# Forward substitution in the second attention layer: probabilities as the stationary operand, one product per later block, one chain in place of two half chains

## The chip, the core and the metric

The kernel runs on one core of one Trainium2 chip. The metric is the device time of one execution in microseconds (us). All of it is one program: two attention layers, a ternary feed-forward layer and a mixture of eight experts, for 4 sequences of 256 tokens with 256 channels. The engines are named as in the profile: PE (TensorE, with PEld for its weight loads), DVE (VectorE), ACT (ScalarE), POOL (GpSimd) and SP (SyncE, here the DMA queue).

## The reference, cut to the part that is changed

The change lies in the second attention layer. It has 16 heads of 16 channels. Besides the usual softmax attention it solves one lower triangular system per head and sequence:

```python
beta = hidden_states @ Wb + bb
s = einsum('bihd,bjhd->bhij', k, k) * scale          # keys against keys
s = where(strict, s, -inf)                           # j < i only
p = e / denom                                        # softmax over j < i
L = p * beta.transpose(0, 2, 1)[..., None]
A = L + eye(T)
u = solve_triangular(A, v, lower=True)               # T = 256 rows, 16 channels
attn = softmax(causal q k^T * scale)
o = einsum('bhij,bhjd->bihd', attn, u)
return o @ Wo
```

So `u = v - L u` in the strictly lower part: row i of `u` needs all earlier rows.

## The kernel before

**Blocks.** The 256 rows are cut into `NS` = 8 blocks of `BLK` = 32. The 128 partitions hold 4 groups of 32 rows (`HQ` = 4, index `hh`), and the free dimension holds 4 heads (`Q4` = 4, index `q`), so a tile of 128 x (4 x 16) is one block of `u` for all 16 heads. Each group of 32 partitions uses its own 32 x 32 tile of the PE array, so four products run side by side.

**What is prepared for a sequence b.** `kscores` makes the key scores in 5 groups, DVE takes their maxima and ACT turns them into sums of exponentials (`ncc`, later `-beta / sum`). `kdiag` makes the diagonal blocks, and POOL inverts all of them in the step `blocks` (lines 1968 to 1984, 62 small operations one after another). DVE transposes the inverses into `invT` in the step `inverse` (line 1754). `kprobs` makes the unnormalised probabilities `later[b % 2][s]`: for block s, keys of that block on partitions, all later queries (7 blocks down to 1) on the free axis. `vproj` makes the right-hand side `vz`.

**The substitution.** For s = 0 to 7 the step `solve` multiplies the inverse of diagonal block s with the right-hand side `zz` (16 products of 32x32 by 32x16), and DVE copies the result from PSUM into `ublk`. Then the step `update` adds the contribution of block s to all later blocks at once: `ublk` is the stationary operand, and `later` streams through with (7 - s) x 32 columns, down from 224 to 32 (line 1104). The result lies in PSUM with channels on partitions, so DVE first transposes the next block's piece (line 1762) and then, head by head, multiplies by `ncc` and adds `vz` (line 1765, four operations). Both steps are split into two halves of two heads each (`half`), which follow each other on PE and DVE. A solution block goes by 4 DMAs from `ublk` to `uaug` (line 831), which `pv` needs complete.

**PSUM.** Each step's PSUM banks come from three rings. `solve` takes turns with `max` and `kmax` in the ring "small" (banks 6 and 7). The running updates lie in banks 4 and 5, one per half.

**Order.** Engines run in the order of `ORDER`, and DVE in `DVE_ORDER`. `make_order` spreads other work (`ahead[b]`: queries, key scores, probabilities and output projection of neighbouring sequences) over the 15 places between the steps of the substitution. The function `lag` lets DVE do a step of the substitution first and the other step that stood ahead of it afterwards. After the substitution of sequence b come `pv` (attention times `u`), then `otr`, `oT`, `wo` (two transposes and the output projection), which are part of the next sequence's spread work. The inversion on POOL for sequence b + 1 starts behind `inverse` for b, since DVE runs `den` and `blocks` for b + 1 there.

## Time and profile before

| | us |
|---|---|
| median of 3 runs (845.45 to 848.48) | 846.26 |
| the profiled execution, its own time | 847.45 |
| its span in the trace | 845.6 |
| first substitution with the work around it | 445.9 to 502.2 |
| move of the last block, first `pv` of the layer | 502.2 to 522.7 |
| second substitution | 522.7 to 579.4 |
| third substitution, POOL inverts the blocks of the last sequence | 579.4 to 628.6 |
| last substitution | 628.6 to 654.7 |
| rest of the layer, experts, output | 654.7 to 845.6 |

The time that the table's first line gives is what is measured from run to run; the trace belongs to the one profiled execution. Its span leaves out 1.85 us around the program. In the rows below, a time is counted from the start of the span. In a row of the timeline, several like instructions that follow each other are merged (x32 is their count), and a matmul on fp32 data stands for two records, so 16 products are x32.

### The profile page before, as it was taken

The page shows a single profiled execution, that of the slowest core. Times are in us where ns is not written, and L with a number is a line of the kernel's source. Part 1 is how long each engine was busy: PE and PEld are TensorE (multiplying, and loading weights), DVE is VectorE, ACT ScalarE, POOL GpSimd, SP SyncE. Part 2 cuts the span into 40 slices and gives each one's busy share as a digit, 9 for nine tenths or more (in the row PEclk, how much of TensorE's full clock was granted, in tenths as well). Part 3 has the DMA queues.
Part 4 walks back from the last instruction along what each step waited for, and adds up shares of the span by engine and source line. Part 5 has one row for each costly group of instructions (what it writes and reads, how often), then busy time and mean ns, then how long its engine had stood idle before and what let it go on. Part 6 is the DMA issues. An engine that isn't in the chain of part 4 may idle for free. (4 is left out here: it accounts for less than half of the span.)

```text
span 845.6 us, 17910 instructions
## 1 busy us (share of the span) xinstructions
PE 506.5 (60%) x7444; PEld 419.3 (50%) x7444; DVE 552.5 (65%) x1066; ACT 299.8 (35%) x716; POOL 227.6 (27%) x320
## 2 busy tenths in 40 slices
PE   0333256288695866426466465758877660899980
PEld 0332144266484645325354344546655450899970
DVE  6549789687699796776627763556564155667733
ACT  3222535244354630053650332442313150365520
POOL 2000000000000000103855826813850026044343
PEclk9865568699788967757677676857979655899995
DMA  8255001404000010760070014200001062656214
GB/s 312 91 112 112 1 1 32 81 1 102 12 2 1 1 50 1 158 143 4 2 151 7 8 43 79 46 6 9 10 9 12 5 276 80 250 193 234 84 52 124
DMA packets 52067, 61.30 MB, mean 72 GB/s; under 512 B 25409, under 2 KB 45393, under 8 KB 47505
## 3 DMA queue, kind: packets, MB, share of 16 engines
q1 hardware_dynamic: 50176, 55.15, 24.2%
q0 software_dynamic: 1808, 4.99, 2.0%
q8 instruction: 59, 0.97, 0.5%
q14 instruction: 24, 0.19, 0.1%
HBM read 45.24 MB, written 13.63 MB: 70 GB/s over the span
## 5 line engine op out<-in xcount | busy, mean ns | idle before, releaser
L873 PE MATMUL psum<-arena 32*32 32x16 f32 (+17 forms) x5608 | 351.3, 269 | 257.3 <-DVE arena L1544 67.1
L873 PEld LDWEIGHTS psum<-arena 128*32 128x32 f32 (+7 forms) x5608 | 279.3, 127 | 328.3 <-DVE arena L1544 70.7
L1979 POOL TENSOR_TENSOR arena<-arena 128x31 f32<-128x31 f32 (+15 forms) x124 | 69.1, 558 | 9.7
L1977 POOL TENSOR_TENSOR arena<-arena 128x31 f32<-128x31 f32 (+15 forms) x124 | 63.6, 513 | 9.7
L1615 DVE TENSOR_REDUCE arena<-psum 128x2 f32<-128x512 f32 (+1 forms) x48 | 41.4, 861 | 21.5 <-PE psum L873 21.1
L1335 ACT ACTIVATE psum<-psum,arena 128x256 f32<-128x256 f32 (+7 forms) x128 | 45.8, 371 | 22.2 <-DVE arena L1605 22.2
L1957 POOL DMA_DIRECT2D arena<-wq x1 | 0.9, 862 | 191.7 <-PE psum L873 191.7
L1304 ACT ACTIVATE arena<-psum 128x512 f32<-128x512 f32 (+1 forms) x48 | 35.3, 735 | 47.0 <-PE psum L873 46.9
L1514 DVE TENSOR_TENSOR_SCAN arena<-arena 128x255 f32<-128x255 f32 x64 | 42.5, 727 | 9.6 <-ACT arena L1247 9.4
L1990 POOL TENSOR_TENSOR fc_second_parts<-arena,fc_first_parts 128x2048 fp32r<-128x2048 f32 x6 | 27.9, 4654 | 63.7 <-ACT fc_first_parts L1425 63.7
L1412 ACT ACTIVATE psum<-psum,arena 128x256 f32<-128x256 f32 x64 | 24.8, 458 | 48.1 <-PE psum L873 48.1
L1762 DVE STREAM_TRANSPOSE arena<-psum 128x64 f32<-128x64 f32 x56 | 13.8, 246 | 42.7 <-PE psum L1104 42.3
L1425 ACT ACTIVATE fc_first_parts<-arena 128x2048 fp32r<-128x2048 f32 x16 | 30.4, 1919 | 26.6 <-PE psum L873 26.6
L1247 ACT ACTIVATE arena<-arena 128x255 f32<-128x255 f32 x64 | 27.2, 500 | 34.9 <-DVE arena L1500 34.9
L1500 DVE TENSOR_TENSOR_SCAN arena<-arena 128x256 f32<-128x256 f32 x64 | 39.0, 671 | 0.4
L873 PE MATMUL psum<-input_first_parts,fc_first_parts 128*128 128x256 f32 x128 | 37.2, 291 | 2.6 <-DVE input_second_parts L1865 1.5
L873 PE MATMUL psum<-fc_first_parts,hidden_first_parts 128*128 128x256 f32 x128 | 36.9, 288 | 2.7 <-DVE hidden_second_parts L1883 2.7
L1997 POOL DMA_INDIRECT dispatched<-arena x16 | 20.3, 1267 | 67.4 <-DVE arena L1830 62.8
L1970 POOL TENSOR_TENSOR arena<-arena 128x1024 f32<-128x1024 f32 x4 | 7.7, 1913 | 110.6 <-DVEq L1747 110.6
L873 PE MATMUL psum<-input_first_parts,fc_second_parts 128*128 128x256 f32 x128 | 36.9, 288 | 0.0
L873 PE MATMUL psum<-input_second_parts,fc_first_parts 128*128 128x256 f32 x128 | 36.9, 288 | 0.0
L1104 PE MATMUL psum<-arena 32*32 32x224 f32 (+6 forms) x896 | 35.9, 307 | 1.5 <-DVE arena L1776 1.5
(180 smaller groups left out, 955.7 us busy)
## 6 DMA issues: line engine op xcount, KB each, us to landing
arena<-fc SPq DMA_DIRECT2D x16, 1024.0 KB, 5.2
arena<-parts SPq DMA_DIRECT2D x40, 256.0 KB, 4.6
parts<-arena SPq DMA_DIRECT2D x16, 384.0 KB, 3.3
arena<-parts SPq DMA_DIRECT2D x40, 128.0 KB, 5.6
dispatched<-arena SPq DMA_DIRECT2D x1, 2048.0 KB, 19.0
arena<-arena SPq DMA_DIRECT2D x128, 8.0 KB, 1.8
arena<-dispatched SPq DMA_DIRECT2D x8, 256.0 KB, 3.1
expert_rows<-arena SPq DMA_DIRECT2D x8, 256.0 KB, 2.2
```

The costliest lines, as they stand in the source:

```text
L873: return nc.tensor.matmul(out, lhsT, rhs, start=start, stop=stop)
L1104: last = nc.tensor.matmul(acc(half)[rows, qq, (s + 1) * BLK:T], ublk[rows, s, q, :], later[b % 2][s][rows, q, :], start=s == 0 and qq == 0 ...
L1247: A(scan[s + 1][:, ct, 0:T - 1], scan[s][:, ct, 0:T - 1], ACT.Copy, scale=back[:, i:i + 1]).then_inc(scaled, 1)
L1304: step_(A(prob[:, hs, 0:T], hi, ACT.Exp, scale=scale))
L1335: ins = A(s_, s_, ACT.Exp, bias=nbias[:, n:n + 1], accum_out=ncc[b][:, n:n + 1])
L1425: A(w_parts[i][e % 2][0][:], fcw[e % NW][i], ACT.Copy).then_inc(w_first, 1)
L1500: ins = V.tensor_tensor_scan(scan[s][:, ct, :], dd, src[:, ct, bt(b)], 0.0, ALU.mult, ALU.add)
L1514: st(V.tensor_tensor_scan(scan[s][:, ct, T - 2::-1], dd, scan[s + 1][:, ct, T - 2::-1], scan[s][:, ct, T - 1:T], ALU.mult, ALU.add))
L1615: st(V.tensor_reduce(mneg[:, H + j * n:H + (j + 1) * n], hi, axis=AX.X, op=ALU.max, negate=True))
L1977: link(G_.tensor_tensor(tmp, A3[:, k + 1:BLK, k:k + 1].to_broadcast([P, rows, w]), X3[:, k:k + 1, 0:w].to_broadcast([P, rows, w]), ALU.mult))
L1979: ins = G_.tensor_tensor(X3[:, k + 1:BLK, 0:w], X3[:, k + 1:BLK, 0:w], tmp, ALU.add)
L1990: G_.tensor_tensor(second[:], fcw[e % NW][1], first[:].bitcast(F32), ALU.subtract).then_inc(w_second[1], 1)
```

## The change

The substitution keeps its blocks and its order of steps, but is formulated the other way around. An `update` for a block is now 16 small products with `later` (32x32) as the stationary and `ublk` (32x16) as the streamed operand, so the result already lies as the solution does, and the transposes go. The update for the next block (s + 1) is made at once; those for the later blocks t > s are made behind `solve` of step s, from block s - 1. The right-hand side is no longer added on DVE: PE multiplies the inverse with `vz` as soon as the update is issued and adds the inverse times the scaled update afterwards in the same PSUM columns (bank 5). DVE is left with one multiplication and one copy per block, each over all four heads. The two half chains become one. `solve` no longer takes part in the ring "small", and `ublk` is 16 columns wide per head instead of 32, without its zeroed half.

```diff
-    ("solve", None): ("small", ("dve",)),
...
-        solve = [[("inverse", b)] + ([("den", b + 1), ("blocks", b + 1)] if b + 1 < B else []) + [("solve", b, 0, 0), ("solve", b, 0, 1)]]
+        solve = [[("inverse", b)] + ([("den", b + 1), ("blocks", b + 1)] if b + 1 < B else []) + [("solve", b, 0)]]
         for s in range(1, NS):
-            solve += [[(kind, b, s - (kind == "update"), half) for half in range(2)] for kind in ("update", "solve")]
+            solve += [[("update", b, s - 1)], [("solve", b, s)]]
...
+            def add_block(b, s, t):
+
+                for q in range(Q4):
+                    for hh in range(HQ):
+                        rows = slice(hh * BLK, (hh + 1) * BLK)
+                        at = (t - s - 1) * BLK
+                        last = nc.tensor.matmul(acc[rows, t, q, :], later[b % 2][s][rows, q, at:at + BLK], ublk[rows, s, q, :],
+                                                start=s == 0 and t == 1 and q == 0, stop=True, skip_group_check=True)
+                return last
+
+            def inverse_of(b, s, first, rhs):
+
+                for q in range(Q4):
+                    n = s * Q4 + q
+                    for hh in range(HQ):
+                        rows = slice(hh * BLK, (hh + 1) * BLK)
+                        last = nc.tensor.matmul(sol[rows, s, q, :], invT[b % 2][rows, n * BLK:(n + 1) * BLK], rhs[rows, q, :],
+                                                start=first and q == 0, stop=True, skip_group_check=True)
+                return last
...
                 elif kind == "update":
 
-                    _, b, s, half = step
-                    wait_done(pe, ("solve", b, s, half), "dve")
+                    _, b, s = step
+                    pe.wait_ge(u_ready, sol_count(b, s))
                     if s == 0:
                         wait_done(pe, ("kprobs", 1, b, KP - 1), "act")
-                        if b == 0:
-                            pe.wait_ge(pad_ready, 1)
-                    for qq in range(QP):
-                        q = half * QP + qq
-                        for hh in range(HQ):
-                            rows = slice(hh * BLK, (hh + 1) * BLK)
-                            last = nc.tensor.matmul(acc(half)[rows, qq, (s + 1) * BLK:T], ublk[rows, s, q, :],
-                                                    later[b % 2][s][rows, q, :], start=s == 0 and qq == 0, stop=True,
-                                                    skip_group_check=True)
-                    last.then_inc(acc_written, 1)
+                    add_block(b, s, s + 1).then_inc(acc_written, 1)
+                    inverse_of(b, s + 1, True, vz[b][:, s + 1])
                 elif kind == "solve":
...
                     else:
-                        pe.wait_ge(z_ready, z_count(b, s, half))
-                    slot = acquire(step)
...
+                        pe.wait_ge(z_ready, z_count(b, s))
+                        inverse_of(b, s, False, zz).then_inc(solved, 1)
+                        for t in range(s + 1, NS):
+                            add_block(b, s - 1, t)
...
                 elif kind == "update":
 
-                    _, b, s, half = step
-                    qs = slice(half * QP, (half + 1) * QP)
-                    dve.wait_ge(acc_written, upd_count(b, s, half))
-                    link(V.transpose(accn[:, qs], acc(half)[:, :, (s + 1) * BLK:(s + 2) * BLK]))
-                    for q in range(half * QP, (half + 1) * QP):
-                        n = (s + 1) * Q4 + q
-                        ins = V.scalar_tensor_tensor(out=zz[:, q], in0=accn[:, q, 0:HD], scalar=ncc[b][:, n:n + 1],
-                                                     in1=vz[b][:, s + 1, q], op0=ALU.mult, op1=ALU.add)
...
+                    _, b, s = step
+                    dve.wait_ge(acc_written, upd_count(b, s))
+                    scale = ncc[b][:, (s + 1) * Q4:(s + 2) * Q4].unsqueeze(2).to_broadcast([P, Q4, HD])
+                    V.tensor_tensor(zz, acc[:, s + 1], scale, ALU.mult).then_inc(z_ready, 1)
                 elif kind == "solve":
-                    _, b, s, half = step
-                    slot = filled(step)
+                    _, b, s = step
+                    dve.wait_ge(solved, sol_count(b, s))
                     if b and s == 0:
                         dve.wait_ge(u_moved, 16 * HQ * NS * b)
-                    give_back(step, V.tensor_copy(ublk[:, s, half * QP:(half + 1) * QP, 0:HD],
-                                                  single(slot)[:, 0:QP * HD].rearrange("p (q e) -> p q e", q=QP)))
+                    V.tensor_copy(ublk[:, s], sol[:, s]).then_inc(u_ready, 1)
```

PE, last substitution (b = 3), from the first update to the second, before. L1104 is the update, L1047 the transposes of `otr`, `32x16` the product with the inverses, and the four rows 128x256 to 128x128 x5 are a group of probabilities:

```order
L1104 MATMUL psum<-arena 32x224 x16
L1047 MATMUL psum<-arena 128x128 x8
L873 MATMUL psum<-arena 32x16 x16
L873 MATMUL psum<-arena 128x256
L873 MATMUL psum<-arena 128x128
L873 MATMUL psum<-arena 128x256
L873 MATMUL psum<-arena 128x128 x5
L1104 MATMUL psum<-arena 32x192 x16
```

The same stretch of PE after the change. L886 is `add_block`, L896 `inverse_of`:

```order
L886 MATMUL psum<-arena 32x16 x16
L896 MATMUL psum<-arena 32x16 x16
L1069 MATMUL psum<-arena 128x128 x8
L896 MATMUL psum<-arena 32x16 x16
L886 MATMUL psum<-arena 32x16 x96
L875 MATMUL psum<-arena 128x256
L875 MATMUL psum<-arena 128x128
L875 MATMUL psum<-arena 128x256
L875 MATMUL psum<-arena 128x128 x5
L886 MATMUL psum<-arena 32x16 x16
```

Six products per head and group (x96) now stand between the second `solve` and the second update; the number falls to 80, 64, 48, 32 and 16 in the steps that follow.

DVE, the end of the last substitution, before, from the copy of block 6 to the copy of block 7 (L1657 and L1544 are the end of `wo` and the gate that follows it):

```order
L1776 COPY arena<-psum 128x2x16 x2
L1762 STREAM_TRANSPOSE arena<-psum 128x64
L1765 SCALAR_TENSOR_TENSOR arena<-arena 128x16 x2
L1762 STREAM_TRANSPOSE arena<-psum 128x64
L1765 SCALAR_TENSOR_TENSOR arena<-arena 128x16 x2
L1657 TENSOR_TENSOR arena<-psum,arena 128x2x256
L1544 SCALAR_TENSOR_TENSOR arena<-arena 128x2x256
L1776 COPY arena<-psum 128x2x16 x2
```

The same stretch of DVE after the change:

```order
L1779 COPY arena<-psum 128x64
L1773 TENSOR_TENSOR arena<-psum,arena 128x64
L1668 TENSOR_TENSOR arena<-psum,arena 128x2x256
L1555 SCALAR_TENSOR_TENSOR arena<-arena 128x2x256
L1779 COPY arena<-psum 128x64
```

The two transposes and four products of a block became one operation, and the other work kept its place.

## Rows read from the trace of the kernel before

**Rows 1.** Engines by stage: window in us, then each engine's busy us (x instructions), granted clock
```profile
445.90:502.20 56.30, 35.37 (x946) 26.04 (x946) 40.20 (x113) 13.02 (x68) 37.05 (x65) 0.70 0.06 7
522.70:579.40 56.70, 37.76 (x1001) 28.64 (x989) 31.84 (x104) 22.25 (x87) 27.97 (x50) 0.72 0.13 21
579.40:628.60 49.20, 39.07 (x870) 29.49 (x870) 30.22 (x89) 13.85 (x29) 37.77 (x66) 0.83 0.08 9
628.60:654.70 26.10, 22.18 (x564) 16.56 (x564) 13.23 (x63) 7.74 (x18) 0.00 (x0) 0.93 0.11 11
```

**Rows 2.** Chain that ended last, by line, in 445.9:502.2, 522.7:579.4 and 628.6:654.7
```profile
by line: PE psum L873 16.0%; ACT psum L1335 15.6%; PE psum L1104 14.0%; DVE arena L1765 8.7%; DVE arena L1615 5.3%; DMA parts<-arena 4.9%; DVE arena L1596 4.3%; DVE arena L1762 3.7%; DVE arena L1754 3.4%; issue 3.2%; DVE arena L1745 3.2%; D
...
by line: PE psum L873 32.7%; ACT psum L1335 12.1%; PE psum L1104 10.4%; DVE arena L1765 9.6%; DVE arena L1596 6.3%; issue 5.5%; DVE arena L1762 4.7%; DVE arena L1615 3.3%; PE psum L1047 1.9%; ACT arena L1349 1.8%; DVE arena L1616 1.8%; DVE 
...
by line: PE psum L873 35.9%; PE psum L1104 21.4%; DVE arena L1765 14.8%; DVE arena L1762 8.5%; DVE arena L1754 7.6%; PE psum L1047 3.9%; issue 3.5%; DVE arena L1544 2.7%; ACT arena L1258 2.4%; PE psum L1057 2.4%; DVE arena L1657 2.3%; DVE a
```

**Rows 3.** The same chain piece by piece: start us, us, what; one block of b = 3
```profile
644.13 0.99 PE psum L873 x24
645.12 0.40 PE psum L1104 x16
645.52 0.02 issue
645.54 0.26 DVE arena L1762
645.80 0.03 issue
645.83 0.38 DVE arena L1765 x2
646.21 0.17 DVE arena L1762
646.38 0.03 issue
646.40 0.39 DVE arena L1765 x2
646.79 0.04 issue
646.84 3.86 PE psum L873 x24
```

**Rows 4.** Timeline of PE: start us, us, instruction xcount, [idle before <-releaser]
```profile
451.08 3.21 PE L1104 MATMUL psum<-arena 32*32 32x224 f32 x32 [1.34 <-DVE arena L1776]
629.38 1.72 PE L1104 MATMUL psum<-arena 32*32 32x224 f32 x32 [0.20 <-DVE arena L1776]
559.09 0.41 PE L873 MATMUL psum<-arena 32*32 32x16 f32 x16
640.73 0.31 PE L873 MATMUL psum<-arena 32*32 32x16 f32 x16 [0.35 <-DVE arena L1765]
504.67 1.60 PE L873 MATMUL psum<-arena 98*32 98x32 bf16 x136 [2.74 <-DVE arena L1565]
562.17 2.65 PE L873 MATMUL psum<-arena 32*32 32x16 f32 x32 [2.67 <-ACT arena L1294]
623.34 4.32 PE L873 MATMUL psum<-arena 128*32 128x256 f32 x64 [0.35 <-issue]
```

**Rows 5.** Durations by line on DVE: x count, ns min/median/max
```profile
L1776 DVE COPY arena<-psum x64: 173/191/193, 450.8 to 654.5; 128x32 f32<-128x32 f32 x64
...
L1723 DVE TENSOR_TENSOR arena<-psum,arena x8: 164/169/175, 343.4 to 507.0; 128x16 f32<-128x16 f32 x8
...
L1562 DVE TENSOR_TENSOR arena<-psum,arena x8: 681/692/693, 334.3 to 502.4; 128x512 f32<-128x512 f32 x8
```

**Rows 6.** Timeline of POOL and DVE: the inversion for the last sequence, first and last pieces
```profile
584.52 1.91 POOL L1970 TENSOR_TENSOR arena<-arena 128x1024 f32<-128x1024 f32 x1 [30.01 <-DVEq L1747]
...
626.66 1.98 DVE L1754 STREAM_TRANSPOSE arena<-arena 128x1024 f32<-128x1024 f32 x1 [4.04 <-POOL arena L1979]
```

**Rows 7.** Chain that ended last, end of the first stage to the first pv
```profile
502.18 2.77 DMA parts<-arena
...
512.11 5.66 DMA arena<-arena
517.77 0.09 issue
517.86 4.21 PE psum L873 x64
```

**Rows 8.** Timeline of SP: the DMAs that move the last block
```profile
654.71 2.52 SPq L831 DMA_DIRECT2D arena<-arena  x4
```

**Rows 9.** Windows around the wait for POOL: columns as in rows 1
```profile
619.50:626.60 7.10, 4.63 (x52) 3.13 (x54) 2.80 (x7) 0.27 (x1) 6.00 (x15) 0.51 0.08 10
...
628.60:631.00 2.40, 2.11 (x64) 1.29 (x64) 0.90 (x6) 0.16 (x1) 0.00 (x0) 1.00 0.04 3
```

**Rows 10.** Groups by line, DVE: x count | busy us, mean ns | idle before, releaser
```profile
L1765 DVE SCALAR_TENSOR_TENSOR arena<-arena 128x16 f32<-128x16 f32 x112 | 27.1, 282 | 2.0
L1762 DVE STREAM_TRANSPOSE arena<-psum 128x64 f32<-128x64 f32 x56 | 13.8, 246 | 42.7 <-PE psum L1104 42.3
L1776 DVE COPY arena<-psum 128x32 f32<-128x32 f32 x64 | 10.6, 187 | 25.7 <-PE psum L873 25.3
```

More of the change, by code:

```diff
@@ L325, in lag @@
         o.append(step)
-        if step[0] == "solve" and step[2] == NS - 1 or not solving:
-            solving = solving and step[-1] == 0
-        if step[0] in ("update", "solve") and step[-1] == 1 or not solving:
+        if step[0] == "solve" and step[2] == NS - 1:
+            solving = False
+        if step[0] in ("update", "solve") or not solving:
             o += held
@@ L625, in later_cols, with per_block @@
             return block_cols(slot, T - (g + 1) * BLK, T - (s + 1) * BLK)
-        def acc(half):
-            return psum[:, 4 + half, :].rearrange("p (q i) -> p q i", q=QP)
+        def per_block(bank):
+            return psum[:, bank, :].rearrange("p (s q e) -> p s q e", s=NS, q=Q4)
+        acc, sol = per_block(4), per_block(5)
         def single(slot):
@@ L822, in _ @@
                     sp.dma_start(wvb[:, :, :, Q4 * HD:VB], d["wb"].rearrange("p c (h n) -> p c h n", h=HQ)).then_inc(loaded["wv1"], 16)
-                elif kind == "solve" and step[3] == 1:
-                    _, b, s, _ = step
+                elif kind == "solve":
+                    _, b, s = step
                     t, r = divmod(s, NB)
-                    for half in range(2):
-                        wait_done(sp, ("solve", b, s, half), "dve")
+                    sp.wait_ge(u_ready, sol_count(b, s))
                     if b and s == 0:
@@ L1112, in _ @@
                         wait_done(pe, ("vproj", b), "act")
-                    else:
-                        pe.wait_ge(z_ready, z_count(b, s, half))
-                    slot = acquire(step)
-                    for qq in range(QP):
-                        q = half * QP + qq
-                        n = s * Q4 + q
-                        for hh in range(HQ):
-                            rows = slice(hh * BLK, (hh + 1) * BLK)
-                            rhs = zz[rows, q, :] if s else vz[b][rows, 0, q, :]
-                            last = mm(single(slot)[rows, qq * HD:(qq + 1) * HD], invT[b % 2][rows, n * BLK:(n + 1) * BLK], rhs)
-                    wrote(step, last)
+                        if b:
+                            pe.wait_ge(u_ready, sol_count(b - 1, NS - 1))
+                        inverse_of(b, 0, True, vz[b][:, 0]).then_inc(solved, 1)
+                    else:
+                        pe.wait_ge(z_ready, z_count(b, s))
+                        inverse_of(b, s, False, zz).then_inc(solved, 1)
+                        for t in range(s + 1, NS):
+                            add_block(b, s - 1, t)
                 elif kind == "route":
@@ L1346, in _ @@
                     else:
-                        wait_pe(act, ("solve", b, NS - 1, 1))
+                        act.wait_ge(solved, sol_count(b, NS - 1))
                         act.wait_ge(invT_ready, b + 1)
```

29 lines of the change are left out of this document (13 added, 16 removed).

## The prediction

> **What bounds the kernel now.** I read the windows by stage first. No engine is full in the stages that hold a substitution: PE is busy 35.4 of 56.3 us in the first and 37.8 of 56.7 us in the second, DVE 40.2 and 31.8 us [rows 1]. Such stages are bound by turns between engines, so the chain of waits decides. Its shares by line [rows 2] give what the substitution holds of each stage, as update (L1104), transpose (L1762) and scale-and-add (L1765) together:
> - first stage: 14.0 + 8.7 + 3.7 = 26.4% of 56.3 = 14.9 us
> - second: 10.4 + 9.6 + 4.7 = 24.7% of 56.7 = 14.0 us
> - last: 21.4 + 14.8 + 8.5 = 44.7% of 26.1 = 11.7 us
>
> The rest of the chain is queries, key scores and probabilities on PE (L873), ACT's exponentials over key scores (L1335) and DVE's maxima (L1596, L1615). It stays.
>
> The third stage is another case. POOL starts to invert the last sequence's blocks at 584.52, and DVE waits 4.04 us for it until 626.66 [rows 6]. Ahead of it stand only two transposes of DVE (about 2 us each). A faster third substitution ends earlier and waits longer, so the 49.2 us of this stage stay, and nothing is gained in it. The way from the first substitution to the first pv is a chain of DMAs (2.77 us of storing, loads, then 5.66 us until the moved block lands behind them) and is not touched either [rows 7]: it only starts earlier. For the first and second sequence POOL is not late: an inversion takes 42 us (584.5 to 626.6) [rows 6], and the stages are 56 us long.
>
> **Price of a product.** 8 products of 32x32 by 32x16 took 0.41 us at 559 and 0.31 us at 640; the 224-column update took 3.21 and 1.72 us [rows 4]. The granted clock around the two cheap ones was 0.93 to 1.00 (2.4 GHz), in the other stages it was mixed, 0.70 and 0.72 [rows 1, 9]. Read as twice the pace and a fixed end, 8 products are 0.10 us + 0.21 at 2.4 GHz and 0.20 + 0.21 at 1.2 GHz. So 16 products that somebody waits for are 0.41 (0.62) us, and 16 that merely stand in the row 0.21 (0.42) us. All 28 narrow products of a sequence are 5.9 us at 2.4 GHz. The seven old updates were 896 columns, at 1.49 us for 224, so 6.0 us. **PE saves nothing.** It even pays for the right-hand side, 7 x 0.21 = 1.5 us per sequence, which lies beside DVE's scaling. What changes is where the work stands. On the chain a block now has only its first product; the far ones (6, 5, 4, 3, 2, 1, in all 21) stand behind the solve, where DVE copies for about 0.4 us. What exceeds that is on the chain when the next step has nothing else to wait for.
>
> A page disagrees. The Trainium skill, "TensorE: Matmul & The Clock Gate", section "Wait — 56ns, not 53.3ns?", says that matmuls never start less than about 25 ns apart, however narrow. By that the 32 records of 16 products would be 0.8 us instead of 0.21. The row of 16 records in 0.31 us speaks against it for products on four tiles of the array [rows 4], and the new ones are of the very same form, so the row is taken.
>
> An upper bound in a long run is the row of 136 records in 1.60 us, 12 ns each [rows 4]: 0.38 us for 16 products. That row has other shapes (98 rows, bf16), the row of like form is nearer, and I take 0.21 and 0.42 and keep 0.38 for the range at 2.4 GHz. Below 0.21 there is no row.
>
> **Price of the scaling.** One DVE operation from PSUM on 64 columns: 16 columns took 169 ns, 512 columns 692 ns, so about 0.22 us [rows 5]. With its wait some 0.25 us, in place of two transposes and four operations, 1.26 us on the chain in the block shown [rows 3]. The copies of 32 columns (191 ns, twice) become one of 64, near 0.22 us: no difference that counts. On the chain the solve's half of 8 products becomes a whole of 16, +0.10 (0.20) us per block.
>
> **Stage by stage** (gain = removed - put back).
> - *First.* PE runs mostly at 1.2 GHz where the updates are. Two updates at 0.41 and five at 0.62 make 3.9, seven scalings 1.75, the solves +1.0. Of the far products, the six of the first block are open: at 1.2 GHz 2.5 us less 0.4. The later ones lie beside the maxima on DVE (0.6 + 0.4 us per group) and the exponentials. 14.9 - 3.9 - 1.75 - 1.0 - 2.1 = **6.1 us**.
> - *Second.* Three updates at 0.41, four at 0.62: 3.7; scalings 1.75, solves +1.0. Open far products: 0.9 + 0.7 in the first two, where only probabilities stand, and 0.4 in the next-to-last two, in all 2.0. One more gain: `solve` leaves the ring "small". At 562 PE waited 2.67 us for ACT to free the slot of `kmax` [rows 4]; the queries queued behind it need a bank that ACT frees about 1 us earlier, and the products another. I take 1.7. 14.0 - 3.7 - 1.75 - 1.0 - 2.0 + 1.7 = **7.3 us**.
> - *Third.* 0, POOL.
> - *Last.* Here a new cost comes in. `pv` of the third sequence ran at 623.34 for 4.32 us [rows 4], right ahead of the last substitution, and the clock, 0.51 in 619.5 to 626.6, was 1.00 when it began [rows 9]. Now that pv is done some 5 us sooner while POOL ends when it did, and PE stands idle before the last substitution. I let PE begin at 1.2 GHz, for about 6 us. Updates 2 x 0.62 + 5 x 0.41 = 3.3, scalings 1.75, solves +0.8; far products 2.5 - 0.4 (slow), then 0.65, 0.45, 0.25: 3.5; one group of probabilities at the low clock +0.5. 11.7 - 3.3 - 1.75 - 0.8 - 3.5 - 0.5 = **1.8 us**. The product of `wo` (most of 3.86 us [rows 3]) and its gate stay. SP issues the 4 DMAs of a block in 2.52 us [rows 8]; blocks come 2.2 to 3.3 us apart and 4.7 before the last but one, so SP's queue is empty again by the last.
>
> Sum: 6.1 + 7.3 + 1.8 = 15.2 us. The profiled execution took 847.45, so it would be 832.2; the median is 1.2 us lower, 846.26 - 15.2 = **831.1 us**.
>
> **Bounds.** With PE at 2.4 GHz in all of it the put-back terms fall: first stage 14.9 - 2.9 - 1.75 - 0.7 - 0.9 = 8.7, second 8.9, last 11.7 - 2.9 - 1.75 - 0.7 - 2.2 = 4.2, together 21.8 us: 824.5. With 0.38 for each far product at 2.4 GHz and all far products of the first two stages open, 63 x 0.38 less 18 places x 0.4 of cover = 16.7 instead of the 7.6 in the sum: 9 us less gain, 840.
>
> **The rivals.**
> - *The chain was not the bound.* In the first two stages ACT's exponentials and DVE's maxima hold 25% of the chain between them, and what is taken out from between might leave them waiting for the same bank. Then only the last stage and the ring's 1.7 us count, 3.5 us: 842.8. For it: ACT's shares of 15.6 and 12.1% [rows 2]. Against: they follow each other in time with the updates, and the chain passes through both.
> - *Slower: PE becomes the bound at 1.2 GHz.* PE does 1.5 us more per sequence at 2.4 GHz and 3.1 at 1.2. If the shorter, narrower work leaves the clock down for the whole of the last substitution, the terms of its sum change: far products 21 x 0.42 less 6 x 0.4 = 6.4 instead of 3.5, five updates +1.05, the solves +0.8, four more groups of probabilities +2.0, and the right-hand sides on the chain ahead of other work, +1.5. That is 8.3 us more than in the sum, a loss of 6.5 instead of a gain of 1.8. The first two stages, with the same prices, gain 1 and 2 us. 846.26 + 6.5 - 3 = 849.8. It decides from a granted clock of about 0.6 in the last substitution (0.93 before). Against: PE was busy 22.2 of 26.1 us there [rows 1] and will be busy as long in less time.
> - *The issue floor.* At 0.8 us per 16 products, 21 far ones stand open for 17 us in each of three stages, near 40 us more than in the sum: over 870. The Trainium skill's page named above gives this rule; the like row speaks against it.
>
> **Chances.** Forecast 0.80, hidden 0.10, slower by the clock 0.09, floor 0.01. About 0.5%, 4.2 us, is what a measurement of this kernel can tell from no change. Faster by more, below 842.0: 0.81 (the forecast, and a little of the hidden case). Within it: 0.10. Slower: 0.09. The range goes from the bound below to the edge of the hidden case: 824.5 to 841.5.
>
> **What would show it.** Right: from the first solve to the last move the stages are about 50, 20.5, 49, 49 and 24 us; DVE's busy time falls by some 38 us (27.1, 13.8 and 10.6 us of L1765, L1762 and L1776 [rows 10] against 60 operations of 0.22); DVE's wait for POOL before the last inverse grows from 4 us to 9; the chain has 0.4 to 0.6 us pieces where the updates stood; PE's idle time behind `kmax` is gone. Wrong: far products (L886) over 0.3 us per 16 at 2.4 GHz; a clock under 0.6 in the last substitution; the third stage shorter than 49 us, which would mean that POOL was not its floor; the second stage still 56 us, with ACT or DVE in place of the updates.

## The result and the profile after

| | us |
|---|---|
| kernel before, median in the same comparison | 846.77 |
| changed kernel, median of 4 runs (888.98 to 899.50) | 892.75 |
| ratio, 95% interval | 1.055 (1.048 to 1.062) |
| profiled execution after, its own time and its span | 894.48, 892.7 |

The change makes the kernel 46 us slower; the prediction said 15 us faster (831.1 us). From one `inverse` of DVE to the next (the places where [rows 6] ends, one for each sequence), then to the last copy of a solution and to the end, the two spans divide as follows. The column "e1" is the changed kernel without its far products, the first experiment below.

| stretch | before | after | e1 |
|---|---|---|---|
| start to the first inverse | 445.9 | 447.8 | 448.5 |
| first substitution, move, first `pv` | 61.4 | 66.4 | 56.5 |
| second | 72.1 | 81.1 | 63.8 |
| third | 47.3 | 59.5 | 46.9 |
| last inverse to the last copy | 27.7 | 50.6 | 27.1 |
| rest | 191.3 | 187.3 | 187.2 |

Every stretch with a substitution is longer, and the last one, where little else runs, by most. Windows over the last substitution from its first copy to its last, of after (columns: stretch, length, busy us and instructions of PE, PEld, DVE, ACT, POOL, granted clock, DMA share, GB/s), answering the last of [rows 1]:

```profile
662.10:705.60 43.50, 34.42 (x1428) 28.91 (x1428) 5.61 (x19) 7.88 (x18) 0.00 (x0) 0.61 0.08 9
```

The same stretch of before:

```profile
629.10:654.60 25.50, 21.77 (x542) 16.16 (x532) 13.17 (x62) 7.47 (x17) 0.00 (x0) 0.93 0.11 12
```

DVE has 7.6 us less to do, as planned. PE has 886 more records of products and 12.7 us more busy time, at a granted clock of 0.61 instead of 0.93. Windows from inverse to inverse, after:

```profile
447.80:514.10 66.30, 46.75 (x1978) 39.04 (x1978) 36.00 (x80) 13.91 (x69) 36.36 (x65) 0.55 0.10 19
514.10:595.30 81.20, 56.32 (x2093) 45.77 (x2093) 27.14 (x68) 26.23 (x93) 36.65 (x65) 0.61 0.20 37
595.30:654.80 59.50, 50.87 (x1701) 42.43 (x1701) 18.47 (x46) 13.13 (x27) 37.43 (x66) 0.59 0.07 9
```

In the third stage PE is busy 50.9 of 59.5 us. Before it was 38.1 of 47.3. The groups by line of after, answering [rows 10] and [rows 4] (busy, mean ns, then the idle time before them and its releaser):

```profile
L886 PE MATMUL psum<-arena 32*32 32x16 f32 x3584 | 57.8, 203 | 18.1 <-issue 16.2
L1773 DVE TENSOR_TENSOR arena<-psum,arena 128x64 f32<-128x64 f32 x28 | 6.3, 224 | 93.3 <-PE psum L886 93.2
L896 PE MATMUL psum<-arena 32*32 32x16 f32 x1920 | 36.0, 204 | 7.9 <-issue 4.8
```

L886 is the product of a block (next or far), L896 the product with the inverse, L1773 the scaling. DVE's scaling takes its 224 ns and waits 93.2 us in all for L886; the first operation of a block before the change waited 42.3 us [rows 10]. And PE stands idle before its own products for a reason called "issue": nothing the profile shows is waited for. The waits of PE over the whole of the substitutions say how much, first before, then after (engine, line, releaser: us in total, times, longest):

```profile
PE psum L873 <- issue: 1.6, 2, 1.3
```
```profile
PE psum L886 <- issue: 16.2, 14, 2.3
PE psum L875 <- issue: 12.8, 9, 2.1
PE psum L896 <- issue: 4.8, 6, 1.2
```

1.6 us in 2 pieces became 33.8 us in 29 pieces. Where these pieces lie is seen in the timeline of PE, last substitution, after (start, us, instruction, count, [idle before <- releaser]):

```profile
683.25 0.93 PE L886 MATMUL psum<-arena 32*32 32x16 f32 x54 [0.56 <-issue]
684.11 1.11 PE L1079 MATMUL psum<-arena 128*128 128x128 f32 x4
685.16 0.62 PE L886 MATMUL psum<-arena 32*32 32x16 f32 x32
685.61 0.82 PE L896 MATMUL psum<-arena 32*32 32x16 f32 x38
687.15 0.55 PE L896 MATMUL psum<-arena 32*32 32x16 f32 x25 [0.72 <-issue]
687.50 0.22 PE L886 MATMUL psum<-arena 32*32 32x16 f32 x3
687.55 0.21 PE L896 MATMUL psum<-arena 32*32 32x16 f32 x1
687.55 1.48 PE L886 MATMUL psum<-arena 32*32 32x16 f32 x93
688.97 1.03 PE L875 MATMUL psum<-arena 98*128 98x256 bf16 x6
690.90 0.39 PE L875 MATMUL psum<-arena 98*128 98x128 bf16 x2 [0.90 <-issue]
```

Count the records from one piece to the next: 54 + 4 + 32 + 38 = 128, and 25 + 3 + 1 + 93 + 6 = 128. Each record of a product has one of a weight load beside it, so 256 instructions lie between two pieces, in the middle of a group of like products, whatever these are. After 690.90 the next counted piece comes at 697.84, another 2 x 128 records later. The page's part on DMA queues has a queue for instructions; before and after:

```profile
q8 instruction: 59, 0.97, 0.5%
```
```profile
q8 instruction: 86, 1.41, 0.7%
```

A transfer is 16 KB (1.41 MB / 86). PE and PEld have 14888 instructions before (7444 each) and 22056 after (11028 each), which is 252 and 256 for each transfer. So this queue brings PE's instructions, 256 at a time. Count PE's recorded instructions from the start of the trace, its semaphore instructions too: 28 of the 29 pieces of after stand at the same remainder of 256, to two instructions. The other one (0.86 us at 656.08) does not, and every kernel here has such a piece ahead of the third sequence's `pv` (0.35 to 3.3 us).

**What ends a piece.** The trace has the time of every transfer of this queue. Before the first seven pieces of the last substitution after the change they landed at 666.61, 670.31, 674.03, 678.17, 681.84, 685.73 and 689.57, and PE went on at 667.89, 671.74, 675.48, 679.50, 683.25, 687.15 and 690.90, each time 1.28 to 1.45 us after the landing; the next transfer began 1.05 to 1.26 us after that. The 13 kernels of this document together have 222 pieces of "issue" in their substitutions. 208 stand at such a boundary, and they end 0.96 to 1.64 us (median 1.40) after the landing of the transfer for that block. At the 371 boundaries without such a piece PE was never earlier than 1.19 us after the landing. So in none of the 13 traces did PE enter a block of 256 instructions earlier than about 1 us after it landed, and the idle pieces are the wait for that.

The consequence is a price for a block, whatever is in it. Where two boundaries in a row had a piece, in any of the 13 kernels, they were 3.3 to 5.9 us apart (median 3.75, 93 pairs). From 667.89 to 690.90 PE went through six blocks, 768 product records:

```profile
667.89:690.90 23.01, 17.01 (x768) 14.63 (x768) 1.35 (x6) 3.21 (x7) 0.00 (x0) 0.52 0.07 9
```

That is 3.84 us for 128 records, or 0.96 us for the 32 records of 16 products. As an estimate, the 1428 records of the whole last substitution are 11.2 blocks, 41.8 us at the median of 3.75, of the 43.5 measured; the 542 records before the change are 4.2 blocks, 15.9 us of 25.5. Before, the delivery of instructions had room; after, it sets the pace of this stretch.

### The profile page after: what moved, and what is told of

Its sections match the earlier page's. It is cut to its first block and busy times, and to the rows that moved or that the text cites. A ratio compares the mean times of both kernels' runs of the same rounds, so it can differ in the third digit from the quotient of the medians.

```text
span 892.7 us, 24810 instructions
## 1 busy us (share of the span) xinstructions
PE 561.5 (63%) x11028; PEld 475.0 (53%) x11028; DVE 516.3 (58%) x894; ACT 300.1 (34%) x716; POOL 224.9 (25%) x319
## 3 DMA queue, kind: packets, MB, share of 16 engines
q8 instruction: 86, 1.41, 0.7%
## 5 line engine op out<-in xcount | busy, mean ns | idle before, releaser
L875 PE MATMUL psum<-arena 98*128 98x256 bf16 (+20 forms) x4584 | 358.4, 295 | 230.6 <-DVE arena L1555 68.7
L875 PEld LDWEIGHTS psum<-arena 96*32 96x32 bf16 (+5 forms) x4584 | 280.1, 132 | 295.4 <-DVE arena L1555 71.9
L886 PE MATMUL psum<-arena 32*32 32x16 f32 x3584 | 57.8, 203 | 18.1 <-issue 16.2
L886 PEld LDWEIGHTS psum<-arena 32*32 32x32 f32 x3584 | 51.7, 140 | 27.0 <-issue 24.1
L1773 DVE TENSOR_TENSOR arena<-psum,arena 128x64 f32<-128x64 f32 x28 | 6.3, 224 | 93.3 <-PE psum L886 93.2
L1346 ACT ACTIVATE psum<-psum,arena 128x256 f32<-128x256 f32 (+7 forms) x128 | 45.7, 370 | 25.6 <-DVE arena L1616 24.8
L896 PE MATMUL psum<-arena 32*32 32x16 f32 x1920 | 36.0, 204 | 7.9 <-issue 4.8
```

The lines of the kernel that those rows point to most:

```text
L875: return nc.tensor.matmul(out, lhsT, rhs, start=start, stop=stop)
L886: last = nc.tensor.matmul(acc[rows, t, q, :], later[b % 2][s][rows, q, at:at + BLK], ublk[rows, s, q, :], start=s == 0 and t == 1 and q == ...
L896: last = nc.tensor.matmul(sol[rows, s, q, :], invT[b % 2][rows, n * BLK:(n + 1) * BLK], rhs[rows, q, :], start=first and q == 0, stop=True ...
L1346: ins = A(s_, s_, ACT.Exp, bias=nbias[:, n:n + 1], accum_out=ncc[b][:, n:n + 1])
```

## The experiments

**Theory I: it is the number of PE's instructions.** A product on fp32 data is two loads and two matmul records, so 16 products are 64 instructions. A substitution had 960 of these (240 products) before and has 2752 (688 products) after, 1344 of them far ones. They take PE's time one by one, and PE is through a block of 256 before the next is at hand. **Theory II: it is the work in the array or the form of the chain**, that is streamed columns, one chain in place of two, or the order.

### e1: no far products

```diff
-                        for t in range(s + 1, NS):
-                            add_block(b, s - 1, t)
```

> The changed kernel without the far products (later blocks t > s + 1 get nothing from block s; that part of the solution is left out). Two theories share the blame differently, and both want the time back here. Theory I (instructions): a far product costs because PE has to be given 4 instructions for each fp32 product (two loads, two matmuls), and these arrive at a limited rate; the gaps with releaser issue go with them. Theory A (array): a far product costs its time in the array at 1.2 GHz. Both: last substitution (first copy to last copy) 20 to 23 us instead of 43.5, total 822 to 836 us. If the total stays above 860, the far products are not the cause and the new order of the chain is.

Measured: 830.08 us (828.52 to 831.65), ratio 0.980 (0.975 to 0.984). The last substitution in its window, first copy to last:

```profile
618.30:642.90 24.60, 21.12 (x756) 17.35 (x756) 5.60 (x19) 7.46 (x17) 0.00 (x0) 0.77 0.12 13
```

The total is within the 822 to 836 us expected; the last substitution is over its 20 to 23. So the far products alone make 63 us. All else that the change does is worth 16 us. That this is near the forecast for the whole (15.2) is chance: the forecast had taken off 7.6 us for the far products, so without them it stood at 22.8. PE busy falls by 13.3 us against after, and PE's idle pieces of "issue" in this window from 8.1 us (8 pieces) to 2.5 (3 pieces); these 13.3 and 5.6 us are the whole of the 18.9 us between 43.5 and 24.6. They are not two separate costs: where every block ends in a wait for the next, a shorter busy time would only make the wait longer. The third stage is back at 46.9 us, with POOL as its floor; DVE waits 8.4 us for it (4.04 before [rows 6]):

```profile
615.58 1.91 DVE L1763 STREAM_TRANSPOSE arena<-arena 128x1024 f32<-128x1024 f32 x1 [8.38 <-POOL arena L1978]
```

### e2: the far products of four heads in one

```diff
-                            add_block(b, s - 1, t)
+                            for hh in range(HQ):
+                                rows = slice(hh * BLK, (hh + 1) * BLK)
+                                at = (t - s) * BLK
+                                nc.tensor.matmul(acc[rows, t], later[b % 2][s - 1][rows, 0, at:at + BLK], ublk[rows, s - 1], ...)
```

> The changed kernel with the far products of the four heads of a row group in one product: the stationary operand of head 0 for all, 64 columns streamed instead of 4 times 16. The columns streamed stay the same, the instructions of the far products fall to a quarter (1344 to 336 per sequence). The values are wrong (one head's probabilities for four). Theory I: the issue gaps in the last substitution (8 us after the change) nearly vanish, last substitution 22 to 26 us, total 828 to 842. Theory A: the array is as busy as before, last substitution 35 us or more, total above 870.

Measured: 835.95 us (834.18 to 837.73), ratio 0.987 (0.981 to 0.992). As many columns are streamed as in the changed kernel, in a quarter of the instructions (and of the weight loads), and 57 of the 63 us are gone. The last substitution kept more of it than the 22 to 26 us expected: 30.2 us from copy to copy.

### e3: the far products on the upper halves of their numbers

```diff
-                            add_block(b, s - 1, t)
+                                    nc.tensor.matmul(acc[rows, t, q, :], later[b % 2][s - 1][rows, q, at:at + BLK].bitcast(BF16)[:, 1::2],
+                                                     ublk[rows, s - 1, q, :].bitcast(BF16)[:, 1::2], ...)
```

> The changed kernel with the far products on the upper halves of the fp32 words (bf16, stride 2): one load and one matmul instead of two of each, so half the instructions (672 per sequence), and one pass in the array instead of four. Theory I: about half of what the far products cost comes back, last substitution 29 to 34 us, total 850 to 866. Theory A: three quarters or more of it come back, last substitution 25 to 27, total 835 to 845.

Measured: 853.43 us (851.77 to 854.71), ratio 1.008 (1.005 to 1.012). With 0, 336, 672 and 1344 far instructions the time is 830, 836, 853 and 893 us. It rises faster than the count, so a fixed price per instruction doesn't describe it either: the first 336 cost 6 us in all, the last 672 cost 0.015 us each in every one of the four sequences (39.3 us / 672 / 4).

### e4: the kernel before, with as many products added

```diff
                     wrote(step, last)
+                    if half == 1 and s:
+                        for t in range(s + 1, NS):
+                            for q in range(Q4):
+                                for hh in range(HQ):
+                                    ...
+                                    nc.tensor.matmul(acc(q // QP)[rows, q % QP, 0:HD], later[b % 2][s - 1][rows, q, at:at + BLK],
+                                                     zz[rows, q, :], start=False, stop=True, skip_group_check=True)
```

> The kernel before, with the same number of products of 32x32 by 32x16 as the far products of the change, at the same places (behind the second half of solve), into PSUM columns that nobody reads. The output is not changed. Theory I: the old kernel slows nearly as the changed one did, though its form, its two half chains and its DVE work are as they were: last substitution 38 to 44 us, total 885 to 905. If instead the new form is what hurts (products in the stationary form, one chain), the old kernel takes the added products at their array price, 63 open ones of 0.2 to 0.4 us: total 855 to 870.

Measured: 892.70 us (886.29 to 899.11), ratio 1.053 (1.035 to 1.072). The old form with two half chains, its transposes and its ring loses 46 us as well, so the new form is not needed for the loss. (The same number of products costs 63 us in the new form, which had 16 us less to begin with.) PE's waits there:

```profile
PE psum L1130 <- issue: 14.3, 9, 2.4
PE psum L873 <- issue: 10.4, 7, 2.3
PE psum L1104 <- issue: 2.2, 2, 1.5
```

L1130 are the added products.

### e6: the same instructions, a quarter of the columns

```diff
-                            add_block(b, s - 1, t)
+                                    nc.tensor.matmul(acc[rows, t, q, 0:4], later[b % 2][s - 1][rows, q, at:at + BLK],
+                                                     ublk[rows, s - 1, q, 0:4], ...)
```

> The changed kernel with its far products cut to the first 4 of their 16 streamed columns (so 12 of 16 columns of every sum miss the far blocks' contribution); the number of TensorE instructions and of weight loads stays. Together with e2 (same columns, a quarter of the instructions, 836 us) this is the other corner. Theory I (instructions): 880 to 900 us, as the changed kernel. Theory II (time in the array, which falls with the columns): 835 to 860 us.

Measured: 896.62 us (894.26 to 898.98), ratio 1.061 (1.055 to 1.068). It is the other corner to e2, and nothing is gained. A row of such products beside the like row of after (693.83, 1.35 us, x64 in both):

```profile
693.23 1.33 PE L1138 MATMUL psum<-arena 32*32 32x4 f32 x64
```
```profile
693.83 1.35 PE L886 MATMUL psum<-arena 32*32 32x16 f32 x64
```

Both rows run at 1.2 GHz (granted clock 0.50) and hold a block boundary at the same place. Rows without one say the same: from start to start a record takes 13.3 ns with 4 columns and 13.4 with 16 at 1.2 GHz, 8.8 and 8.7 ns at 2.4 GHz (medians of the long rows). Four streamed columns take as long as sixteen. Theory II, as streamed columns, falls, and with e4 so does the form of the chain. One rival inside Theory I is left open: every product has a weight load, so no run tells the number of instructions from the number of loads as the price of a record in a row. The wait at the boundary goes by instructions, since it stands at multiples of 256 of them.

### e5: the right-hand side added by DVE

```diff
-                    inverse_of(b, s + 1, True, vz[b][:, s + 1])
...
-                        inverse_of(b, s, False, zz).then_inc(solved, 1)
+                        inverse_of(b, s, True, zz).then_inc(solved, 1)
...
-                    V.tensor_tensor(zz, acc[:, s + 1], scale, ALU.mult).then_inc(z_ready, 1)
+                    link(V.tensor_tensor(zz, acc[:, s + 1], scale, ALU.mult))
+                    V.tensor_tensor(zz, zz, vz[b][:, s + 1], ALU.add).then_inc(z_ready, 1)
```

> The changed kernel with one part undone: VectorE adds the right-hand side to the scaled sum (one more TENSOR_TENSOR on the chain), and TensorE does not put it in beforehand. That takes 7 x 16 = 112 products, 448 instructions of TensorE, out of each sequence, and adds 28 operations of about 0.22 us with their hand-over, some 9 us. Theory I (what costs is the number of TensorE instructions in a row): the four runs before gave about 0.06 us per instruction and sequence between 672 and 1344 far ones, so 448 fewer are worth up to 27 us: 865 to 885 us. Theory II (the products of the right-hand side run while VectorE scales and are hidden, so they cost nothing): the added operation alone is seen, 898 to 905 us.

Measured: 876.51 us (873.35 to 879.67), ratio 1.037 (1.031 to 1.044). One more operation on the chain of DVE, 28 times, and it is 16 us faster, because 448 instructions per sequence are gone from PE. The forecast had called the right-hand side on PE free beside the scaling.

### e7: do the small moves delay the instructions?

```diff
-                        sp.dma_start(uaug[r * BLK:(r + 1) * BLK, t, ...], ublk[hh * BLK:(hh + 1) * BLK, s, :, :]
+                        sp.dma_start(uaug[r * BLK:r * BLK + 1, t, ...], ublk[hh * BLK:hh * BLK + 1, s, :, :]
```

> The changed kernel with the solution's moves cut to one row in 32 (4 packets and not 128 per transfer; the other rows never reach the last product, so the output differs). It tells whether TensorE's idle time that waits for nothing the profile shows, 8.1 us in 8 pieces in the last substitution, each at a multiple of 128 product records, comes from these small packets standing in the way of the instruction transfers. If it does: the pieces fall below 3 us there and the time to 870 to 885 us. If it does not (Theory I alone): 887 to 900 us with pieces as before.

Measured: 896.97 us (893.79 to 900.14), ratio 1.058 (1.048 to 1.068). The idle pieces stay, 7.5 us in 9 in the last substitution. The packets of the moves are not their cause.

### c1: the old orientation, the next block first, the rest in wide products

```diff
-                    add_block(b, s, s + 1).then_inc(acc_written, 1)
+                    add_block(b, s, 0, BLK).then_inc(acc_written, 1)
...
+                    if 0 < s < NS - 1:
+                        add_block(b, s - 1, BLK, T - (s + 1) * BLK)
...
-                    V.tensor_tensor(zz, acc[:, s + 1], scale, ALU.mult).then_inc(z_ready, 1)
+                    link(V.transpose(accn, acc[:, :, (s + 1) * BLK:(s + 2) * BLK]))
+                    V.tensor_tensor(zz, accn[:, :, 0:HD], scale, ALU.mult).then_inc(z_ready, 1)
```

> Another form of the same idea, with few products: as before the solution is the weights and the probabilities are streamed, but only the next block's 32 columns ahead of VectorE (16 products); the rest, up to 192 columns in 16 products, stands behind the second application of the inverse, where the changed kernel has its far products. One chain, one transposition of both halves and one scaling on VectorE, the right-hand side added by TensorE. 448 fp32 products per sequence at most (e1 has 352, the changed kernel 688). Theory I (instructions): the first two stages gain most of what e1 gained (13 us), less the transpositions; the last stage is 3 to 6 us longer than before's 25.5, its chain being e1's 3.1 us per block with 0.35 to 0.5 us for the transposition; 834 to 844 us in all. Rival (one chain with the transposition is longer than the two interleaved ones in every stage): 850 to 865 us.

Measured: 846.53 us (840.99 to 853.09), ratio 0.999 (0.996 to 1.003). Neither expectation held. The last substitution was as expected (30.3 us from copy to copy), but the stages from inverse to inverse took 58.6, 71.0 and 47.1 us, so all three together gained 4.2 us and not most of 13. Why the second stage kept 7 us over e1's is not settled; TensorE has 1792 instructions per substitution here against e1's 1408, and 9.5 us of "issue" against 8.4. The granted clock of its last substitution was 0.83 with 948 product records, against 0.72 in e2 with 924.

### c2, c3, c4: fewer instructions in the new form

c2 is e5 and e3 together. c3 has the next block's products on the upper halves as well:

```diff
-                        last = nc.tensor.matmul(acc[rows, t, q, :], later[b % 2][s][rows, q, at:at + BLK], ublk[rows, s, q, :],
+                        last = nc.tensor.matmul(acc[rows, t, q, :], later[b % 2][s][rows, q, at:at + BLK].bitcast(BF16)[:, 1::2],
+                                                ublk[rows, s, q, :].bitcast(BF16)[:, 1::2],
```

c4 leaves the right-hand side on TensorE and has `add_block` and the second application of the inverse on the upper halves.

> Both reductions of TensorE instructions: the right-hand side added by VectorE as in e5_rhs_dve, and the far products on the bf16 upper halves of their numbers as in e3. TensorE then has 1632 instructions per substitution, against 2752 in the changed kernel, 1744 in e2 and 1408 in e1. Theory I (instructions): 832 to 836 us by the count between e1 and e2, and about 9 us for the operation added to the chain, together 836 to 850 us. Theory II (what matters is the far products being there, and the right-hand side is hidden): e3's 853 us and 9 more, 858 to 866 us.

> c2 with the products for the next block on the bf16 upper halves too: 1408 TensorE instructions per substitution (as many as e1 has), 224 fewer than c2, and the 16 products that VectorE waits for are 32 records and not 64 instructions. Theory I (instructions): c2's 839 us less 3 to 8 us, 831 to 837 us. Rival (c2 is already bound by the chain with its added VectorE operation, not by TensorE's instructions): 837 to 841 us.

> The changed kernel (right-hand side added by TensorE) with every product that only carries a correction on the bf16 upper halves: the next block's, the far ones, and the second application of the inverse. 1632 TensorE instructions per substitution, as c2, but no VectorE operation added, and two of the three groups on the chain halved. Theory I (instructions): below c2's 839 us by the 28 VectorE operations that c2 adds (some 8 us) and by the shorter groups (up to 4 us): 827 to 833 us. Rival (the 448 instructions of the right-hand side, which c2 had taken from before each second application, cost here what they cost between e5 and the changed kernel, 16 us): 840 to 850 us.

Measured: c2 839.29 us (833.65 to 842.97), ratio 0.994 (0.991 to 0.997). c3 834.18 us (831.13 to 835.99), ratio 0.983 (0.976 to 0.990). c4 836.27 us (835.45 to 838.45), ratio 0.987 (0.980 to 0.994), which misses its 827 to 833 and its rival's 840 to 850. c3 beats both kernels, at the price of cutting the corrections (not the right-hand side, nor the inverse) to the upper 16 bits of their numbers.

### All of them by the number of instructions

"Instructions" are those of PE in one substitution, worked out from the loops. "Issue" is PE's idle time without a shown reason between the first inverse and the last copy, in us. One piece of 6.8 us in c3 does not stand at a block boundary, and what it waits for is not known.

| kernel | instructions | issue | median, us |
|---|---|---|---|
| before | 960 | 1.6 | 847 |
| e1 | 1408 | 8.4 | 830 |
| c3 | 1408 | 12.8 | 834 |
| c2 | 1632 | 6.3 | 839 |
| c4 | 1632 | 16.0 | 836 |
| e2 | 1744 | 12.1 | 836 |
| c1 | 1792 | 9.5 | 847 |
| e3 | 2080 | 22.6 | 853 |
| e5 | 2304 | 24.3 | 877 |
| e4 | 2304 | 26.9 | 893 |
| changed kernel | 2752 | 33.8 | 893 |
| e6, e7 | 2752 | 36.4, 33.5 | 897, 897 |

With the new chain and up to 1744 instructions the kernel is faster than before; from 2080 on none is. The kernels e1, e2, e6 and e7 leave work out or compute with the wrong numbers, so of those that were faster only c2, c3 and c4 can take the kernel's place.

## Why the prediction was wrong, step by step

**What bounds the kernel.** Right for the kernel before: a chain of turns with PE 63% busy in the first stage. The step from there, "PE saves nothing" and so costs nothing either, was made in busy time at the best pace. The changed kernel was PE's: busy 50.9 of 59.5 us in the third stage, and in the last held by the delivery of its instructions.

**The far products: the step that failed.** The sum gave them 7.6 us: 2.1 in the first stage, 2.0 in the second, nothing in the third and 3.5 in the last. Against e1 they cost 62.7 us: 9.9, 17.3, 12.6 and 23.5 by stage (66.4 - 56.5 and so on), with 0.6 us less elsewhere. Two things were wrong, the second by far the larger.

The price of a record in a row was a little low. For 16 products somebody waits for, 0.41 (0.62) us were predicted, and the rows show 0.44 and 0.62 (x32). For 16 that stand in the row, 0.21 us at 2.4 GHz and 0.42 at 1.2 GHz were predicted, from two short rows read as "twice the pace and a fixed end" [rows 4]. Starts in the trace say 8.5 and 13.4 ns a record, 0.27 and 0.43 us for 16 products: the pace is 1.6 times and not twice, and the end is 0.18 us at the high clock and 0.21 at the low. At 2.4 GHz from start to start, 0.27 us:

```profile
662.41 0.44 PE L886 MATMUL psum<-arena 32*32 32x16 f32 x32 [0.40 <-DVE arena L1779]
662.68 0.45 PE L896 MATMUL psum<-arena 32*32 32x16 f32 x32
```

At 1.2 GHz it is 685.16 to 685.61 in the timeline above, 0.45 us. The longest row,

```profile
664.36 1.57 PE L886 MATMUL psum<-arena 32*32 32x16 f32 x131
667.89 0.70 PE L886 MATMUL psum<-arena 32*32 32x16 f32 x61 [1.96 <-issue]
```

has 1.57 / 131 x 32 = 0.38 us for 16, like the row of 136 other products that the prediction kept for its bound; but that holds the 0.18 us of the last record's end and one halt of 0.16 us. As an estimate, all 84 groups of 16 far products (21 for each sequence) at 0.43 us with nothing hidden are 36 us. So the price of a record, at either clock, does not explain 62.7.

The second is a term that the sum put at nothing: that PE's instructions are at hand whenever it is ready. The row of 131 is followed by 1.96 us in which PE has none. Far products are 1344 of the 2752 instructions of a sequence, 5.25 blocks of 256. At the 3.75 us of a block where the delivery sets the pace that is an estimate of 19.7 us a sequence; the last substitution, where little else runs, lost 23.5. With it fell the cover of 0.4 us each behind DVE's copy: in the last substitution PE waits for DVE in one piece of 0.4 us, and the other 8.1 us of pieces are "issue". The measured bound that the prediction had, 0.38 us for each far product, gives 840 us and misses this too.

**The issue floor**, the rival with a chance of 0.01, named over 870 us and the right side. Its mechanism did not occur: 0.8 us for the 32 records of 16 products is 25 ns from start to start, and they started 8.5 ns apart at 2.4 GHz. Where the delivery set the pace, 16 products took 0.96 us, near its 0.8; that its time came out right is luck. But it was the only case in which a narrow product has a price apart from its columns, and that is what the runs showed.

**What stood against it, and was not seen.** The Trainium skill has in "Runtime: NRT & Kernel Launch", section "Instruction fetch mechanics", that the instructions are refilled in blocks of 16 KiB, 256 each, and that the cost of crossing such a boundary is mostly hidden. The blocks agree with this trace (128 products and 128 loads from piece to piece, 16 KB per transfer). The cover does not: 29 pieces of up to 2.3 us, 33.8 us in all. No run could make the delivery itself faster. That it is the cause rests on the place and size of the blocks, on the fixed time from landing to going on (208 pieces, and none of 371 other boundaries earlier), and on the growth with the count; e7 excludes the packets of the moves.

**The clock rival** gave 849.8 us and the condition "about 0.6 in the last substitution". The condition came true, 0.61. Its price there was 8.3 us more than the forecast's; measured were 18 us lost instead of 1.8 gained, 19.8 more. The clock is a smaller part of it. At the low clock the 21 far groups there cost 21 x 0.16 = 3.4 us more than at the high one (an estimate), and the rest of PE's work, the same in e1, was busy 22.5 us instead of 18.7. And in the six blocks from 667.89 on PE waited for instructions at the end of each although it ran mostly at 1.2 GHz (0.52); a faster clock would have lengthened those waits.

**Third stage.** "0, POOL" failed by 12.2 us on the other side. After, POOL is done long before DVE asks:

```profile
641.88 0.25 POOL L1980 TENSOR_TENSOR arena<-arena 128x31 f32<-128x31 f32 x1
```
```profile
652.01 0.22 DVE L1779 COPY arena<-psum 128x64 f32<-128x64 f32 x1 [1.07 <-PE psum L896]
```

The substitution ended 10 us after POOL. A floor hides gains, not losses. In e1 POOL was the floor again, and DVE waited for it about as the prediction said (8.4 us, 9 predicted).

**DVE.** Right. The scaling took 224 ns and so did the copy (0.22 each predicted), and DVE's busy time fell by 36.2 us (552.5 to 516.3) where 38 were predicted.

**The gain of the chain.** Without its far products the forecast was 8.2 and 9.3 us for the first two stages, 0 for the third and 5.3 for the last, 22.8 in all. e1 shows 4.9, 8.4, 0.4 and 0.6, 14.3 in all. So the chain of turns was a bound in the first two stages, as predicted, and the "hidden" rival falls. The wait of PE behind `kmax`, 3.3 us before (ACT L1294), is gone in e1. The last stage failed here too: e1 has 756 product records in it against 542 before, a clock of 0.77 against 0.93, and 2.5 us of waits for instructions. That the total of e1 is 16 us owes something to another stretch. Behind the last copy the kernels of the new form are 3 to 5 us faster than before, which no step had; e4, of the old form, is faster there too, by 2.5 us, so the new form is not shown as the cause. The product of `wo` there, before and in e1:

```profile
669.13 3.78 PE L873 MATMUL psum<-arena 128*128 128x256 f32 x8 [0.69 <-ACT arena L1356]
```
```profile
656.07 1.99 PE L875 MATMUL psum<-arena 128*128 128x256 f32 x8 [0.69 <-ACT arena L1365]
```

It takes half the time; the granted clock of the 30 us from `pv` on was 0.56 before and 0.73 in e1. The start, 2.6 us later in e1, takes part of this back; it was as late (448.3 us) in e4, the kernel before with products added behind this point, so it is no effect of the change.

## What to carry to other kernels

Count the instructions of an engine and not only the elements: of fp32 products each is four. When a wide product is split into many narrow ones, divide the instructions of the stretch by 256. Here a block cost at least 3.3 us, and 3.75 as a rule, when PE was ready sooner, so a stretch with fewer microseconds than that for each block will wait. An operation that is hidden at its pace in a short row is not hidden when hundreds follow each other. Take the pace of a row from start to start, and not from its length, which holds the end of the last record. When a kernel was bound by turns between engines, check at the low clock that none of them becomes full.

## What the runs showed that was not expected

- PE stood idle for up to 2.3 us at multiples of 256 of its instructions when these were short: 33.8 us in 29 pieces, against 1.6 us in 2 before. It went on 1.23 to 1.56 us after the block's transfer had landed, and the next transfer began 1.0 us or more after that.
- Product records of fp32 on four 32x32 tiles started 8.5 ns apart at 2.4 GHz and 13.4 ns at 1.2 GHz with 4, 16 and 32 streamed columns alike (4 in e6, 16 in after, 32 in before and c1); with 64 columns it was 14.0 and 24.8 ns (before). The bf16 records of e3, 32x16, were 8.4 and 8.5 ns apart, so they lost nothing at the low clock.
- The granted clock of the last substitution was 0.61 after the change with PE busy 34.4 of 43.5 us, against 0.93 before with 21.8 of 25.5. It was at 2.4 GHz from 661.9 to 668.7 and at 1.2 GHz until 702.8; PE had stood idle for 1.96 us shortly before it fell. What decides it is not shown.
